# A gated two-layer transformer block on one core: another layout of the second attention's softmax and value products

## The reference, cut to what matters

```python
q = query_states @ Wq.T + bq
k = key_value_states @ Wk.T + bk
v = key_value_states @ Wv.T + bv
# 16 heads of 8 features, q scaled by 8 ** -0.5
scores = jnp.einsum('bhqd,bhkd->bhqk', q, k)
attn = jax.nn.softmax(scores, axis=-1)
ctx = jnp.einsum('bhqk,bhkd->bhqd', attn, v)
return ctx.transpose(0, 2, 1, 3).reshape(B, SQ, HIDDEN) @ Wo.T + bo
# x = x + tanh(g_xattn[1]) * that
```

## Time and profile before

| | us |
|---|---|
| median of 3 runs | 337.32 |
| profiled execution, its own time | 339.97 |
| its span, first to last instruction | 337.3 |
| PE busy | 296.4 |
| DVE busy | 247.9 |
| ACT busy | 165.1 |
| POOL busy | 103.8 |
| mean granted TensorE clock | 0.969 |

### The profile page before, as it was taken

How to read it: one execution, slowest core, us unless ns; L and a number is a source line. 1 busy time by engine, 2 the same in 40 slices (tenths; PEclk the granted TensorE clock), 3 DMA queues, 4 the chain that set the end, 5 groups by cost and what they waited for, 6 DMA issues and landing times.

```text
span 337.3 us, 5717 instructions
## 1 busy us (share of the span) xinstructions
PE 296.4 (88%) x1488; PEld 222.8 (66%) x1488; DVE 247.9 (73%) x727; ACT 165.1 (49%) x427; POOL 103.8 (31%) x157
## 2 busy tenths in 40 slices
PE   1889879998998999858898898898887999999995
PEld 1677756665766666537787787787874667676662
DVE  2479778976887977654868868868868877958662
ACT  1237653224233242466798797797862233233321
POOL 6216615020055010263529829829401010100000
PEclk9999958999899999987999999999999999999999
DMA  7901104818605125000000000000004233061550
GB/s 216 328 16 38 31 4 153 247 28 256 166 26 176 54 97 157 0 1 0 2 1 3 2 0 0 0 0 1 3 17 154 83 121 116 22 209 36 165 179 31
DMA packets 16279, 26.45 MB, mean 78 GB/s; under 512 B 2789, under 2 KB 5299, under 8 KB 16051
## 3 DMA queue, kind: packets, MB, share of 16 engines
q1 hardware_dynamic: 15448, 24.93, 24.0%
q10 hardware_dynamic: 808, 1.25, 1.3%
HBM read 24.29 MB, written 1.25 MB: 76 GB/s over the span
## 4 chain that ended last, share of the span: by engine, by line
PE 54%; DVE 17%; ACT 8%; DMA 7%; issue 6%; SPq 3%; POOL 2%; DVEq 1%; ACTq 0%; POOLq 0%
PE bank L547 20%; PE Ybank L569 13%; DMA CR<-comb_rows 4%; PE bank L722 4%; ACT PX L977 3%; DVE cmx L1327 2%; DVE xn L1088 2%; PE Tb L471 2%; DMA comb_rows<-ct 2%; DVE st L1074 2%; SPq L295 1%; DMA CB<-in_consts 1%; DVE recT L1343 1%; SPq L302 1%; DVE xl L1094 1%
## 5 line engine op out<-in xcount | busy, mean ns | idle before, releaser
L890 ACT ACTIVATE sg<-bank 128x512 f32<-128x512 f32 x64 | 38.1, 597 | 76.6 <-PE bank L547 59.4
L334 POOL TENSOR_TENSOR rstd<-ve,mhalf 128x4 f32<-128x4 f32 x16 | 16.2, 1011 | 162.2 <-DVE ve L1081 162.2
L1227 DVE TENSOR_TENSOR hb<-sg,CR 128x512 f32<-128x512 f32 x64 | 44.9, 703 | 18.4 <-DMA CR<-comb_rows 8.4
L1220 DVE TENSOR_TENSOR sg<-sg,bank 128x512 f32<-128x512 f32 x64 | 43.5, 680 | 6.7 <-PE bank L547 4.2
L1327 DVE TENSOR_REDUCE cmx<-bank 128x4 f32<-128x308 f32 x64 | 28.3, 472 | 17.5 <-PE bank L695 17.2
L342 POOL TENSOR_TENSOR KS<-kr,CB 128x1232 fp32r<-128x1232 f32 x16 | 36.1, 2260 | 11.3 <-PE bank L695 11.3
L547 PE MATMUL bank<-xh,WBH 128*128 128x512 f32 x68 | 36.2, 533 | 1.2 <-DVE sg L1220 0.6
L547 PE MATMUL bank<-xh,UPH 128*128 128x512 f32 x64 | 36.2, 566 | 0.0
L569 PE MATMUL Ybank<-hb,W2T 128*128 128x512 f32 x64 | 33.5, 604 | 3.1 <-DVE hb L1227 3.1
L569 PE MATMUL Ybank<-hb,downw 128*128 128x512 f32 x64 | 33.0, 599 | 0.4 <-DVE hb L1227 0.3
L977 ACT ACTIVATE PX<-bank,cmx 128x77 f32<-128x77 f32 x128 | 29.4, 355 | 0.0
(11 more groups left out here) (179 smaller groups left out, 612.0 us busy)
## 6 DMA issues: line engine op xcount, KB each, us to landing
CR<-comb_rows SPq DMA_DIRECT2D x64, 128.0 KB, 3.0
CR<-comb_rows SPq DMA_DIRECT2D x32, 256.0 KB, 3.4
VX<-in_vs_seed SPq DMA_DIRECT2D x4, 320.0 KB, 4.6
w13raw<-in_w SPq DMA_DIRECT2D x1, 1088.0 KB, 11.6
X<-in_x SPq DMA_DIRECT2D x4, 256.0 KB, 9.5
upraw<-in_up SPq DMA_DIRECT2D x4, 256.0 KB, 4.7
out_x<-X SPq DMA_DIRECT2D x4, 256.0 KB, 3.6
cT<-in_ctxT SPq DMA_DIRECT2D x4, 154.0 KB, 6.1
```

Of the source, the lines that this page charges most:

```text
L334: nc.gpsimd.tensor_tensor(rstd[:], ve[:], mhalf[:], ALU.pow).then_inc(rstd_rdy, 1)
L890: A(sg[:, k % 2, :], Gb[k % 2][:], ACT.Silu).then_inc(m.s_done, 1)
L1220: V.tensor_tensor(sg[:, k % 2, :], sg[:, k % 2, :], Ub[k % 2][:], ALU.mult).then_inc(m.t2, 1)
L1227: V.tensor_tensor(hb[:, k % 2, :], sg[:, k % 2, :], CR[:, k % RING, :], ALU.mult).then_inc(m.h_done, 1)
```

## The change

It rewrites the tile's softmax and value products, and puts the work of the second attention in another order on PE, ACT and DVE.

- The four score slices get four banks, in one array S4. DVE takes the maxima of two slices in one instruction (616 columns), and centres both in one; all slices are now centred by DVE, and ACT exponentiates 616 columns at once.
- The transposed probabilities become the stationary operand and the values move: VX holds, for each chunk, its heads' 8 values and a column of ones (9 columns a head) in a field of 128 columns that is zero elsewhere. The output has tokens on partitions, with each head's sum in its ninth column.
- DVE takes the reciprocal of 128x16 sums and multiplies in one instruction. The result is then transposed by PE (`c_turn`), copied by ACT (`c_turned`), and projected, all one tile late. pt is doubled; context, turned context and projection share one bank.
- VX is zeroed once by POOL, in place of four loads of 320 KB by SP, and the loads of the last stage's weights move forward in their place. The first tile's values are placed before a norm step on POOL.

```diff
-            def c_scores(g, t, s, first=False):
+            def c_scores(g, t, u, first=False):
                 n = GB * g + t
                 if t == 0:
-                    pe.wait_ge(qs_done, NHG * g + s + 1)
-                if s == 0:
+                    pe.wait_ge(qs_done, NHG * g + 2 * u + 2)
+                if u == 0:
                     pe.wait_ge(ks_done, n + 1)
-                    pe.wait_ge(c_sub, len(SUB_EXP) * n)
...
+                if not first:
+                    pe.wait_ge(c_sub, START + NU * n + u - 1)
+                for s in (2 * u, 2 * u + 1):
...
-            def c_mix(g, t, u, first):
+            def c_mix(g, t, first):
 
                 n = GB * g + t
...
+                pe.wait_ge(c_fin, START + n)
+                if first and t == 0:
+                    pe.wait_ge(mB.y_cp, START + NG)
+                pe.wait_ge(vx_rdy, n + 1)
+                pe.wait_ge(c_ev, START + 3 * n + 3)
+                for c in range(NC):
                     w = chunk_rows(c)
-                    v = (t % 2 * NC + c) * P
-                    i = mm(bOut[t % 2][:, u * P:(u + 1) * P], VX[0:w, v:v + P], pt[0:w, c * P:(c + 1) * P],
+                    i = mm(bO9[c // CU], pt[0:w, t % 2, c * P:(c + 1) * P], VX[0:w, t % 2, c, :],
                            start=c % CU == 0, stop=c % CU == CU - 1)
...
+            def c_turn(g, t):
+                n = GB * g + t
+                pe.wait_ge(c_norm, START + n + 1)
+                pe.wait_ge(c_otc, START + n)
+                tr(bOT, On[:].rearrange("p h d -> p (h d)"), I).then_inc(c_ot, 1)
...
+            def c_turned(g, t):
                 n = GB * g + t
-                act.wait_ge(c_pv, START + n + 1)
-                act.wait_ge(c_rs, START + n)
-                A(sumT[0:UD, :], bOut[t % 2][UD:P, 0:P], ACT.Copy)
-                A(sumT[UD:P, :], bOut[t % 2][0:UD, P:2 * P], ACT.Copy).then_inc(c_sum, 1)
+                act.wait_ge(c_ot, START + n + 1)
+                act.wait_ge(c_wo, START + n)
+                A(OTs[:], bOT, ACT.Copy).then_inc(c_otc, 1)
...
             def c_normalize(g, t):
                 n = GB * g + t
-                dve.wait_ge(c_rs, START + n + 1)
-                dve.wait_ge(c_wo, START + n)
...
+                dve.wait_ge(c_pv, START + n + 1)
+                V.reciprocal(share, mixed[:, :, :, HD]).then_inc(c_rs, 1)
+                dve.wait_ge(c_rs, n + 1)
+                dve.wait_ge(c_ot, START + n)
+                V.tensor_tensor(On[:].rearrange("p (u h) d -> p u h d", u=NU), mixed[:, :, :, 0:HD],
+                                share.unsqueeze(3).to_broadcast([P, NU, UH, HD]), ALU.mult).then_inc(c_norm, 1)
```

More of the change, by code:

```diff
@@ L755, in c_body @@
-                    if end:
+                    before = (g, t - 1) if t else None if first else (g - 1, GB - 1)
+                    if t < GB - 1:
+                        c_scores(*n1, 0)
+                    c_transpose(g, t, 0)
+                    if t == GB - 1 and not last:
+                        c_scores(*n1, 0)
+                    if before:
+                        c_turn(*before)
+                    if t == GB - 1 and not last:
+                        c_repeat(g + 1, 2)
+                    c_transpose(g, t, 1)
@@ L757, in c_body @@
+                    if before:
+                        c_project(*before)
+                    if t < GB - 1:
+                        c_scores(*n1, 1)
+                    elif not last:
+                        c_repeat(g + 1, 3)
+                    else:
                         pe.wait_ge(up_split, 8)
                         pe.wait_ge(in_up, 96)
-                        pe.wait_ge(c_exp, NHG * NB)
+                        pe.wait_ge(c_sub, START + NU * NB)
                         m_gate(mD, 0, 0)
@@ L761, in c_body @@
                         m_linear(mD, 0, 0)
-                    if ahead:
-                        c_scores(*n1, 3)
                     if t == 2 and not last:
                         c_repeat(g + 1, 0)
-                    c_mix(g, t, 0, first)
+                    c_transpose(g, t, 2)
+                    if t == 1:
+                        if last:
+                            m_logits(mD, 0)
+                        else:
+                            c_query(g + 1)
+                    if t == GB - 1:
+                        if last:
+                            m_route_T(mD, 0)
+                        else:
+                            c_scores(*n1, 1)
@@ L773, in c_body @@
                         c_repeat(g + 1, 1)
-                    if end:
-                        m_gate(mD, 0, 1)
-                        c_project(g, t - 1)
-                    c_mix(g, t, 1, first)
-                    if t == 2 and not last:
-                        c_repeat(g + 1, 2)
             def c_ahead(k):
@@ L1035, in _ @@
             m_y_copy(m, NG - 1)
-            for s in range(NHG):
-                c_exps(0, 0, s, first=True)
+            for u in range(NU):
+                c_exps(0, 0, u)
             c_body(0, True, False)
@@ L1394, in c_body @@
                         route_pick(mD, 0)
-                    if t == 0 and first:
-                        m_update(mB, NG - 1, Tb)
-                    if end:
-                        c_final(g, t - 1)
             def c_ahead(k):
@@ L1442, in laid_out @@
     across = lambda v: _np.broadcast_to(v.reshape(-1, 1), (P, P))
-    seed = _np.zeros((P, NC * P), _np.float32)
-    for h, c, row, _, n in value_pieces():
-        ones = c * P + (1 - h // UH) * UD + h % UH * HD
-        seed[row:row + n, ones:ones + HD] = 1.0
     heads = _np.zeros((P, HG), _np.float32)
```

272 lines of the change are left out of this document (111 added, 161 removed).

## The result

The changed kernel takes 345.12 us in the median of four runs (344.23 to 346.65), the kernel before 337.07; the ratio is 1.023, with a 95% interval from 1.018 to 1.029. Forecast were 343.5 and a range of 338 to 349, so the sign and the size came out. The parts of the sum did not, as the stretches of the changed kernel show. They are the view of the earlier trace rows, with the same columns, cut where the same tiles' value products start: the 1st, 4th, 8th, 12th and 15th tile's, and the first `hb` of the last stage.

The account below looks back on a forecast made before the run. The prediction took a chain hopping between three engines, not busy time, as the bound. Its terms, +3.8 without the DVE-POOL lock and +6.2 with it, on a median of 337.3 gave 343.5 us, range 338 to 349.

Parts of the forecast that it names:

- the step from the fourth tile: Loop, fourth tile's value products to the next tile's: 6.33 us, with statistics and their tail at 1.45.
- The price of the chain: Loop pass laid down instruction by instruction in the new order, without port waits: 26.95 us, +1.9 a pass.
- The second step: Loop, first to second tile's value products: 6.81 us, including centring and the wait for the residual 0.88.
- The third step: Loop, second to third tile's value products: 6.21 us, growing to 8.0 with DVE and POOL locking each other out.
- The fourth: Loop, third to fourth tile's value products: 7.60 us, including an exponential of 0.58.
- The port: Second to third tile: DVE's query split waits behind POOL's keys, 6.2 to 8.0 in both passes, +3.5 in all.
- The rule on ports in the prediction: DVE casts or two-SBUF-input instructions and POOL instructions reading SBUF lock each other out for a whole instruction.
- the same rule costs the old order about 1.2: Old order's DVE and POOL waits, about 1.2 us, taken as already in its trace.
- The first group: Second attention, up to the fourth tile's value products: +1.0 us.
- The last group: Second attention, first three tiles of its last group, after the two passes: +1.6 us.
- The end: After the last value products, to the first `hb`: less work follows and the last tile is shorter, -2.5 us or so.
- Rival 3: Loop: if the exponential doesn't hold the last copy, passes fall toward 22.8, total about 327 to 331 us; chance 0.11.

Follow-up runs that it names:

- The copy alone: Changed kernel with a tile's third copy of transposed probabilities on ACT moved ahead of the next tile's first exponential; 344.93 us, ratio 1.021.
- single slices: Changed kernel with each maximum and centring over 616 columns made by two instructions over 308; 348.25 us, ratio 1.032.
- the run with early statistics: Changed kernel with the norm's statistics on DVE moved from the end of the fourth tile to the end of the third; 339.63 us, ratio 1.006.
- the second trace of the kernel before: The kernel before, not edited, run again for another trace; 337.39 us, ratio 1.000.
- the moves: Changed kernel with statistics early, third transposes and copy forward: 334.47 us; plus last repeated query's copy ahead of the exponential: 331.27; plus norm's low part earlier: 328.11.
- the fastest one: Changed kernel with statistics early, third transposes and copy, last repeated query's copy and norm's low part all moved forward; 328.11 us, ratio 0.970.
- two moves in the old layout: Kernel before with statistics moved to the third tile and, in the second tile, the norm's low part ahead of the centring; 332.66 us, ratio 0.986.

## Why the prediction was right, and where it was not

- **That the chain bounds the stage, and not busy time: right.** The pass grew by 3.2 to 3.3 us with 0.3 more of PE's work and ACT relieved by a quarter.
- **The reason given for it: wrong.** The prediction had it that "the exponential of the next tile stands ahead of the copy on which this tile's products wait". The copy alone moves nothing (345.12 to 344.93); its transposes stand late on PE, behind the projection and scores. Together they are worth 4.1 us. The larger half was named, in the list of the step from the fourth tile, only as a duration of 1.45: the statistics, now in front of a normalising that everything waits for. They are worth 5.5.
- **The price of the chain: too low.** The pass without the lock was laid down at 26.95. The steps of the second pass are 6.90, 7.22, 6.78 and 7.79 for 6.33, 6.81, 6.21 and 7.60: 1.7 more. In the first step of the four, the statistics take 1.86 us to the reciprocal for 1.45 (1.62 in the first pass), and the reciprocal and product 0.50 for 0.41. The second step was laid down over DVE's work on pairs; it is 7.22 with single slices too, so the pairs don't set it. In the trace DVE waits 0.2 for the projection before the residual, and the low part behind that sets the query: the path over the context's transpose, its copy and the projection was priced 0.25 too low, and residual and low part as much again. The third step has the port, 0.56; without it, in the run with early statistics, it is 6.22 for 6.21. The fourth is 0.2 too long, and of that only 0.04 for each exponential is accounted for.
- **The port: right in kind, a third in size.** The step was to grow from 6.2 to 8.0. It grew by 0.77 in the first pass and 0.56 in the second, since the CAST came into the middle of POOL's keys and not ahead of a second instruction of them, and the subtraction followed at once:

```profile
216.06 2.27 POOL L344 TENSOR_TENSOR KS<-kr,CB 128x1232 fp32r<-128x1232 f32 x1
...
217.26 1.34 DVE L1307 CAST qh<-qf 128x512 fp32r<-128x512 f32 x1 [0.47 <-ACT qf L959]
218.64 0.69 DVE L1311 TENSOR_TENSOR ql<-qf,qh 128x512 fp32r<-128x512 f32 x1
219.25 0.25 DVE L1339 RECIPROCAL rec<-Ybank 128x16 f32<-128x16 f32 x1
```

  The keys end at 218.33 and the CAST at 218.60; free of them it takes 0.43. The products had been ready at 218.64, so the normalising lost 0.6. The rule on ports in the prediction (the Trainium skill, "SBUF — State Buffer", Who interferes with whom) agrees: the CAST ends 0.27 behind the whole of POOL's instruction. The other half of this term was wrong: the prediction had it that "the same rule costs the old order about 1.2", and in the old order the CAST takes 0.47 us, and 0.44 once the statistics are early, while the step stays at 5.87 to 5.90.
- **The first group: wrong sign.** +1.0 was forecast and -1.4 measured. The forecast kept the fall of the clock as the first trace has it, 6.8 us long. In the changed kernel it is 3.4 us, as in the second trace of the kernel before. From the first repeat of the query on PE (139.86, 136.35 and 139.79 us) to the 4th tile's products it is 34.99 us in the first trace of the kernel before, 33.72 in the second and 33.65 in the changed kernel. So 1.3 of the miss of 2.4 is the longer fall, which was no property of the old order, and against the second trace the group is level: the +1.0 itself did not come.
- **The last group: +3.8 for +1.6.** Here up to 1.7 (half of 3.4 us) is a new fall of the clock, behind 237.6 us, just as the 13th tile's products have begun:

```profile
237.00:241.00 4.00, 3.53 (x17) 3.56 (x18) 1.01 (x2) 1.04 (x3) 4.00 (x8) 0.58 0.00 0
```

- **The end: right.** -2.05 for -2.5. A part is given back, because PE takes up the context's transpose behind the gates, 0.55 after it was ready (the timeline of the end):

```profile
261.50 0.29 DVE L1342 TENSOR_TENSOR On<-Ybank,rec 128x128 f32<-128x128 f32 x1
...
262.34 0.27 PE L721 MATMUL Ybank<-CB,On 128*128 128x128 f32 x1
...
262.98 0.49 PE L727 MATMUL Ybank<-WXo,OTs 128*128 128x128 f32 x2 [0.37 <-ACT OTs L985]
```

The total came out right by luck, with errors that cancel: a port priced at 3.5 us over two passes where 1.3 show, and a first group of +1.0 with a long fall of the clock kept in it, against a chain priced 1.0 to 1.2 too low in each pass, 1.2 us of lock subtracted for the old order where none shows, and a fall of the clock in the last group. The reckoning of the old passes was itself 0.7 short over two. Rival 3, that relief of ACT and DVE wins, is refuted where it was put (the pass did not fall). Its condition, products that start as soon as PE comes to them, is what the moves bring near, and 328.1 lies in its 327 to 331. But the relief is not what won it in the loop: the old layout, without it, comes to the same pass.

## What to carry to other kernels

Here a rewrite took work off two engines, and the chain through them still grew, since what stood in between had less cover. Before judging a layout, look at what is queued in front of each hop (here the statistics) and move it to where its engine waits. Moving the consumer gained nothing while its producer stood late on its own engine; moving both did. And try the same kind of order in the old kernel: here it came to the same pass, and of the 9.6 us between the kernel before and the fastest one, 4.6 came with two moves in the old layout.

## What the runs showed of the hardware

- Which operand of an fp32 product of 128 by 128 is stationary made no difference here: ten took 2.50 us before and take 2.50 after.
- The clock is at half for 3.4 us at the start of this stage in eleven of twelve traces, and for 6.8 in one. Further stretches of 3.4 us at half came behind 237 us in the changed kernel, and in other traces at 172, 209, 230, 233, 240, 246, 248 or 252, or not at all, in kernels whose passes have PE busy for 78 to 93%; the kernel before has one in one trace of two. At half the clock such a stretch costs up to 1.7 us, a fifth of the effect studied here. What begins or ends them is not settled by these runs.
- Reading two banks in one instruction showed no cost of its own: 0.47 us for 308 columns of one bank, 0.79 to 0.80 for 616 of two, where the line through 0.47 and 0.68 (512 columns of one bank) gives 0.79.
- A CAST of 128x512 from fp32 to fp32r took 0.43 us beside an idle POOL. When it started 0.7 to 1.5 us into POOL's 2.26 us on the keys it took 1.86 down to 1.01, and in all nine such cases in the loop's passes it ended 0.27 to 0.29 us behind POOL.
